# Masking two more attention units by Relu and a select instead of a matrix product

## What is computed

```python
qkv = hidden_states @ w_attn + b_attn
q, k, v = jnp.split(qkv, 3, axis=-1)            # each (B, 1024, 32, 16)
scores = jnp.einsum('bqhd,bkhd->bhqk', q, k) * SCALE
bias = slopes[:, None, None] * rel[None, :, :]  # rel = key position - query position
causal = rel <= 0
scores = jnp.where(causal[None, None], scores + bias[None], -jnp.inf)
attn = jax.nn.softmax(scores, axis=-1)
out = jnp.einsum('bhqk,bkhd->bqhd', attn, v).reshape(B, S, HIDDEN)
return out @ w_proj + b_proj
```

## Time and profile before

| what | value |
|---|---|
| median of 3 runs | 909.03 us (908.92 to 909.49) |
| the profiled execution | 909.71 us |
| its span | 907.5 us |
| PE busy | 852.9 us (94%) |
| DVE busy | 750.5 us (83%) |
| ACT busy | 473.3 us (52%) |
| Pool busy | 301.1 us (33%) |

### The profile page before, as it was taken

The page is one execution under the profiler, slowest core; times in us unless marked ns, Lnnn a source line. Parts: engine busy times, 40 slices in busy tenths (PEclk is TensorE's granted clock), DMA queues, the critical chain, the costliest instruction groups (busy, mean ns, idle before and its releaser), DMA issues.

```text
span 907.5 us, 12065 instructions
## 1 busy us (share of the span) xinstructions
PE 852.9 (94%) x4031; PEld 400.7 (44%) x4031; DVE 750.5 (83%) x1613; ACT 473.3 (52%) x904; POOL 301.1 (33%) x310
## 2 busy tenths in 40 slices
PE   5999878899989999899999999999999999999996
PEld 3435424454447454344444444443444444444442
DVE  5699999999998875888999999995247799767877
ACT  4777654666652032112888888888734555343100
POOL 1057999899984000050121111211110443000000
PEclk8888999999999999999999999999999999999999
DMA  9300060300005015510322202200052000000011
GB/s 345 110 0 1 1 278 0 139 1 1 1 0 206 2 48 182 177 41 6 86 80 81 58 26 79 81 2 3 1 177 73 1 0 1 0 0 1 12 40 41
DMA packets 22135, 54.06 MB, mean 60 GB/s; under 512 B 6085, under 2 KB 12869, under 8 KB 19066
## 3 DMA queue, kind: packets, MB, share of 16 engines
q1 hardware_dynamic: 22074, 53.30, 17.2%
HBM read 44.70 MB, written 8.39 MB: 59 GB/s over the span
## 4 chain that ended last, share of the span: by engine, by line
PE 58%; DVE 8%; SPq 2%; issue 1%; POOL 1%; ACT 1%; DMA 1%; POOLq 0%; DVEq 0%
PE ps L1222 17%; PE ps L1084 7%; PE ps L1233 6%; PE ps L1064 5%; PE ps L1048 3%; PE ps L1051 3%; PE ps L1143 3%; PE ps L1123 3%; PE ps L993 3%; PE ps L1106 2%; SPq L320 2%; DVE ps L1489 1%; DVE mrow L1496 1%; PE ps L802 1%; DVE mrow L1493 1%
## 5 line engine op out<-in xcount | busy, mean ns | idle before, releaser
L481 POOL TENSOR_TENSOR hC<-hs,C_sb 128x512 f32<-128x512 f32 x128 | 160.3, 1270 | 50.9 <-ACT C_sb L685 31.5
L755 ACT ACTIVATE prob<-ps 128x512 f32<-128x512 f32 x288 | 158.9, 602 | 28.3 <-PE ps L1067 12.6
L973 PE MATMUL ps<-hC,identf 128*128 128x512 f32 x256 | 139.1, 646 | 13.4 <-POOL hC L481 12.1
L614 ACT ACTIVATE ps<-dtT,nA 128x512 f32<-128x512 f32 x128 | 88.2, 690 | 50.4 <-DVE hs L1377 47.2
L504 POOL TENSOR_SCALAR_AFFINE_SELECT prob<-prob 128x256 f32<-128x256 f32 x96 | 39.0, 406 | 224.1 <-ACT prob L755 224.1
L1064 PE MATMUL ps<-stack 123*128 123x512 bf16 (+3 forms) x384 | 108.4, 327 | 1.3 <-ACT prob L755 1.1
L1496 DVE TENSOR_REDUCE mrow<-ps 128x1 f32<-128x512 f32 x128 | 81.9, 683 | 7.3 <-PE ps L1051 5.3
L1084 PE MATMUL ps<-prob,V 128*32 128x512 f32 (+3 forms) x768 | 81.6, 498 | 0.7 <-POOL prob L504 0.7
L973 PEld LDWEIGHTS ps<-hC,identf 128*128 128x128 f32 x256 | 47.6, 201 | 72.9 <-POOL hC L481 56.1
L1222 PE MATMUL ps<-hT,wg 128*128 128x512 f32 (+1 forms) x176 | 79.1, 592 | 0.0
L1222 PE MATMUL ps<-hT,wu 128*128 128x512 f32 (+1 forms) x176 | 79.1, 592 | 0.0
(11 more groups left out here) (201 smaller groups left out, 1320.1 us busy)
## 6 DMA issues: line engine op xcount, KB each, us to landing
stack<-parts_dram SPq DMA_DIRECT2D x96, 128.0 KB
wmod<-in_wmod SPq DMA_DIRECT2D x4, 1536.0 KB, 12.5
parts_dram<-qkp SPq DMA_DIRECT2D x16, 384.0 KB, 2.6
wmod<-in_wmod SPq DMA_DIRECT2D x4, 1024.0 KB, 10.5
wattn<-in_wattn SPq DMA_DIRECT2D x1, 3072.0 KB, 10.3
wg<-in_wg SPq DMA_DIRECT2D x1, 2752.0 KB, 11.1
wu<-in_wu SPq DMA_DIRECT2D x1, 2752.0 KB, 10.7
wd<-in_wd SPq DMA_DIRECT2D x1, 2560.0 KB, 10.6
```

Of the source, the lines that this page charges most:

```text
L481: pool.tensor_tensor(hC[:, c, :], hs[:, c, :], C_sb[:, m % 2, :], ALU.mult).then_inc(S["hc_done"], 1)
L614: A_(ps[:, DA_BANK + c % 2, :], dtT[:, c, half(h)], ACT.Exp, scale=nA[:, c * NS + s:c * NS + s + 1]).then_inc(S["da_done"], 1)
L755: A_(prob[:, u % 4, j, :], ps[:, 3 + F % 3, :], ACT.Exp, scale=-1.0).then_inc(S["exp_done"], 1)
L973: mm(ps[:, c, :], identf[:], hC[:, c, :], start=False, stop=(s == NS - 1), skip_group_check=True).then_inc(S["sum_done"], 1)
```

## The change

`PAIRS` now holds every diagonal tile of every unit, whether the unit has one piece or two. So in the units with one diagonal tile ACT does a Relu of 128 columns in PSUM ahead of the exponential, Pool does a select of 128 columns behind it, the weighted values of these units wait for it, and PE's product with `negm` is no longer there. Units 6 and 7 change places: unit 6 is now key block 4 with its diagonal tile, unit 7 is key block 3 without one. `negm` is still loaded and is used for DVE's mask in the first pass.

```diff
@@ -63,13 +63,13 @@
     ((2, 256, 256, 0), (6, 768, 256, 256)),
     ((1, 512, 512, 0),),
     ((2, 512, 512, 0),),
+    ((4, 512, 512, 0),),
     ((3, 512, 512, 0),),
-    ((4, 512, 512, 0),),
     ((5, 640, 384, 0), (7, 896, 128, 384)),
 )
 NU = len(UNITS)
 
-PAIRS = tuple(tuple(col // P for kb, q0, w, col in pieces if q0 == kb * P) if len(pieces) == 2 else () for pieces in UNITS)
+PAIRS = tuple(tuple(col // P for kb, q0, w, col in pieces if q0 == kb * P) for pieces in UNITS)
@@ -500,8 +500,8 @@
                     pool.wait_ge(S["exp_done"], F + 1)
-                    w = prob[:, U % 4, j, :].rearrange("p (n c) -> p n c", c=P)[:, on[0]:on[1] + 1:on[1] - on[0], :]
-                    pool.affine_select(w, w, [[0, 2], [1, P]], ALU.is_ge, 0.0, base=0, channel_multiplier=-1) \
+                    w = prob[:, U % 4, j, :].rearrange("p (n c) -> p n c", c=P)[:, on[0]:on[-1] + 1:max(1, on[-1] - on[0]), :]
+                    pool.affine_select(w, w, [[0, len(on)], [1, P]], ALU.is_ge, 0.0, base=0, channel_multiplier=-1) \
                         .then_inc(S["masked"], 1)
@@ -748,7 +748,7 @@
-                    x = ps[:, 3 + F % 3, :].rearrange("p (n c) -> p n c", c=P)[:, on[0]:on[1] + 1:on[1] - on[0], :]
+                    x = ps[:, 3 + F % 3, :].rearrange("p (n c) -> p n c", c=P)[:, on[0]:on[-1] + 1:max(1, on[-1] - on[0]), :]
@@ -1060,11 +1060,8 @@
                 for kb, q0, w, col in UNITS[u]:
-                    diag = q0 == kb * P and not PAIRS[u]
                     ins = mm(ps[:, bank, col:col + w], qk[0:ATT_ALL, 1, j, tile(kb)], qk[0:ATT_ALL, 0, j, q0:q0 + w],
-                             start=True, stop=not diag)
-                    if diag:
-                        ins = mm(ps[:, bank, col:col + P], identb[:], negm[:], start=False, stop=True)
+                             start=True, stop=True)
                 ins.then_inc(S["st_mm"], 1)
```

## The result

The changed kernel takes 913.17 us (median of 6 runs, 912.06 to 913.59) against 908.97 us before, measured together: a ratio of 1.0045, with an interval of 1.0034 to 1.0056, so slower by 3.1 to 5.1 us. Forecast were 912.2 us, range 908.3 to 914.2, slower with a chance of 0.63.

What follows compares the result with a forecast made beforehand. DVE's row minima were taken to set the pace in groups 0 to 6, PE in the last; 2.6 + 0.3 + 0.5 - 0.24 = +3.2 us on a median of 909.03 gave 912.2 us, range 908.3 to 914.2.

Steps and rivals of the forecast that it cites:

- The bound: Attention: DVE's row minima set the pace in groups 0 to 6, PE in short stretches and the last group; ACT's load uneven.
- Rival B: PE bounds everywhere, so each of 64 mask products removed counts 0.06 us: 909.0 - 3.8 = 905.2 us; chance 0.10.
- The slack of 0.76 us: ACT's free time at the end of a group's first unit, ahead of step 4's Relu: 0.76 us.
- The Relu's price: Each added 128-column Relu on ACT: 263 ns interpolated, 0.30 us start to start, with bounds 0.19 and 0.41 us.
- +0.44 us per group change: Steps 0 to 3: four Relus add 1.20 us, 0.76 free; delay reaches PE and DVE, +2.6 us over six changes.
- Group 0: First group's start: four Relus put step 4's Relu 0.7 us late, 0.55 caught before step 10; +0.3 us.
- Steps 24 to 27 free: Unit 6's four Relus, 1.2 us, fit into ACT's 1.4 us of idle time: cost nothing in groups 0 to 5.
- The sentence on the exchange: Without exchanging the units, the Relus would fall in steps 28 to 31, straight ahead of unit 8's 0.90 us steps.
- Change from group 6 to 7 and the last group: Eight Relus, 2.4 us against 2.0 idle on ACT, cost +0.5 us; four products fewer in the last group gain 0.24.
- Selects: 64 selects of 128x128 on Pool, at most 406 ns each: no difference, since Pool is busy 4.88 of 30 us.
- Rival D: Pool's select of unit 0 or 6 comes after PE wants its values, from 0.6 us of lateness; chance 0.10 with C.

Runs made afterwards that it cites:

- e5: Changed kernel with the new Relus of units 0 and 6 on 4 columns instead of 128, their exponential at scale -0.25; ratio 1.0005 to the kernel before.
- e6: Changed kernel with the new Relus of units 0 and 6 on 256 columns instead of 128; ratio 1.0095 to the kernel before.
- e11: Changed kernel without the Relus of units 0 and 6, their exponential at scale -0.25, repeated for its trace; 908.88 us as a lone execution.
- e4: Changed kernel's unit order, but only unit 6 masked by Relu and select, unit 0 keeping its product; ratio 0.9991 to the kernel before.
- e1: Changed kernel with units 6 and 7 back in the old order; ratio 1.0034 to the kernel before.
- e2: Kernel before with units 6 and 7 exchanged and the mask products kept; ratio 1.0007 to the kernel before.
- e3: Kernel before, old unit order, with only unit 0 masked by Relu and select, unit 6's block keeping its product; ratio 1.0034.
- e8: Changed kernel with ACT's copy of OT after step 7 instead of 5, PE's transposes in step 10 instead of 9; ratio 1.0051 to the kernel before.
- e9: Changed kernel with ACT's copy of OT after step 10, PE's transposes in step 12, DVE's normalisation in step 13; ratio 1.0048 to the kernel before.

## Why the prediction was right

By its steps:

- **The bound.** DVE's pace with short stretches of PE, and ACT's load uneven behind a low average. Borne out: work on ACT reached the period only beyond its slack (e5, e6, e11), and work on PE hardly did. Rival B, each product worth 0.06 us, is out: 64 products fewer without new Relus gave 0.05 us a group (e11).
- **The slack of 0.76 us.** Right to 0.05: three sizes of Relu meet the line there.
- **The Relu's price.** 0.263 us interpolated, 0.271 measured; 0.30 us start to start forecast, 0.31 measured. The Trainium skill's rule (ScalarE: Activation LUTs, section What ACT_TABLE_LOAD costs), 186 ns plus 0.833 ns per column with immediate scale and bias, gives as an estimate 293 ns for 128 columns, 399 for 256 and 189 for 4. The traces show 271 and 377 in the changed kernel and 167 in e5: 22 ns less each time, with the same slope.
- **+0.44 us per group change.** Measured 0.45 on average, 2.67 us in six against 2.6. The size is right, one detail isn't: the text puts PE's wait, "about 0.4 us", at step 9. It is 0.18 us at step 7 and 0.31 at step 9. The pair one turn earlier, step 4's exponential and PE's weight load for step 7, is nearly as tight, and I hadn't written it down: in the kernel before the exponential ends at 549.44 and the load starts at 549.58, 0.14 us later.

```profile
549.58 0.32 PEld L1064 LDWEIGHTS ps<-stack 123*128 123x128 bf16 x2
```

Having stood at step 7, PE comes to step 9 later by itself and waits less there.
- **Group 0**: +0.3 forecast, +0.32 measured; step 4's Relu, forecast 0.7 us late, starts 3.59 us after the first transposed scores (432.63 less 429.04) where it was 2.90 (431.60 less 428.70).
- **Steps 24 to 27 free**: right (e4). The sentence on the exchange suggested that the Relus would be worse off in steps 28 to 31; e1 shows them free there too. The exchange without the Relus would cost 0.18 us a group, since it puts the products into steps 24 to 27 (e2); with the Relus it changes nothing that was measured.
- **Change from group 6 to 7 and the last group**: +0.5 - 0.24 = +0.26 forecast, +0.16 measured. ACT's Relu of step 12 in the last group divides the two, in the kernel before, the changed one and e11:

```profile
641.54 0.37 ACT L753 ACTIVATE ps<-ps 128x256 f32<-128x256 f32 x1 [1.07 <-PE ps L1064]
```

```profile
645.43 0.37 ACT L753 ACTIVATE ps<-ps 128x256 f32<-128x256 f32 x1 [1.07 <-PE ps L1063]
```

```profile
641.30 0.37 ACT L753 ACTIVATE ps<-ps 128x256 f32<-128x256 f32 x1 [1.07 <-PE ps L1063]
```

After the seventh reduction (621.97, 625.30, 621.97) these are 19.57, 20.13 and 19.33 us. So the change from group 6 to 7 costs +0.56 us, near the +0.5; it is made of 0.80 for the new Relus less 0.24 for the missing products. From there to the end the changed kernel and e11 are both 0.40 us shorter than before: the last group's products gave 0.40, not 0.24. The gain of the last group was put too small by 0.16 us.
- **Selects**: nothing, as forecast. They take 292 ns, and PE's wait for Pool is one of 0.7 us in the last unit, as before. Rival D didn't come.

The sum was 3.2 us, the three parts give 3.15. That it came this near is in part luck: six changes, group 0 and the change from group 6 to 7 took 0.07, 0.02 and 0.06 us more than forecast, and the last group 0.16 less, which cancels. The timed ratio says 3.1 to 5.1 us, with 4.1 in its middle. Where a further microsecond would be stays open: in the profiled execution the part ahead of attention is longer by 0.34 us, which varies by more than that between kernels that are the same there, and the part behind it is the same to 0.01 us. e1 and e3, whose parts sum to 3.3 and 3.4 us, both have a ratio of 1.0034, which is 3.1 us; so the 4.1 may be scatter, which no run shows.

## What to carry over

An engine's free time counts where the work is added, not on average: ACT was free for 5 us of each 30, and had 0.76 where four of the new Relus went. The gain of a move is judged the same way: taking a copy out of ACT's chain only let PE reach its next wait for ACT sooner (e8, e9). Before adding work to a lightly loaded engine, follow its timeline to the next point at which another engine waits for it, and take the gap there as the budget; beyond it every nanosecond was paid by all here. And taking work from an engine that looks busy for 99% of the time gave next to nothing where it waits for another in turn (0.05 us a group for eight products), though four products of 0.06 us cost 0.18 us in steps 24 to 27 and nothing four steps on.

## What the runs showed beside this

- Where PE's weight load waited for ACT's exponential, it started 0.05 us after the end of the exponential: at steps 7 and 9 of the changed kernel, at step 10 of e8 and e9, and at step 9 of the kernel before, where the wait was no loss yet.
- The second of two exponentials of 512 columns starts 0.49 us after the first though each takes 0.60; behind a Relu that it waits for, it starts 0.02 to 0.03 us after the Relu's end.
- The stretch ahead of attention took from 426.7 to 429.4 us in executions of kernels that are the same there.
